# Three bias matmuls folded into the residual rows, and row and weight copies dropped, in a transformer kernel with linear attention

## The chip, the cores and the metric

The kernel runs as one program on 1 core of one Trainium2 chip. The metric is device time in microseconds (us), the median of several runs.

## What is computed

The input is 8 sequences of 512 tokens of width 128, in float32. An outer block modulates a layer norm of the input, runs a small transformer over it, and then a mixture of experts. The change touches the small transformer, which has four layers (16 heads of 8 features, feed-forward width 512) and is cut here to what matters:

```
for l in range(4):
    q, k, v = x @ Wq[l] + bq[l], x @ Wk[l] + bk[l], x @ Wv[l] + bv[l]
    att = causal_linear_attention(elu(q) + 1, elu(k) + 1, v)
          # (inter + intra) / (den_inter + den_intra + ATT_EPS), chunks of 128 tokens
    x = x + att @ Wo[l] + bo[l]
    x = layernorm(x) * g1[l] + be1[l]
    y = gelu(x @ W1[l] + b1[l]) @ W2[l] + b2[l]
    x = layernorm(x + y) * g2[l] + be2[l]
return layernorm(x) * gf + bef
```

None of the biases is zero. After it come a residual with a gate, a second modulated layer norm, a router over 16 experts with two chosen for each token, a shared expert and the weighted sum. That part is not changed except for one wait.

## The kernel before

**Tiles.** A tile is 128 tokens by 128 features. A row is one sequence: `NT` = 4 tiles. All 32 tiles of the residual stream stand in SBUF in `X`. There are `STEPS` = 32 pairs of a layer and a row. Every engine has its own program, unrolled by `steps`: it runs `body(k * NT)` for k = -1 to 34, and in one step k the work of four pairs is interleaved: the transposes of x for pair k+1 (`active(i, -1)`), projections and the first two attention tiles for pair k (`back` 0), the other attention tiles, the output projection and the first layer norm for pair k-1 (`back` 1), the first feed-forward matmul for pair k-2 (`back` 2), the second one and the second layer norm for pair k-3 (`back` 3). The first steps also carry the head (the modulated layer norm of the input, a row at a time, `dve_head_step` and its like), the last ones the tail.

**Order.** The order on each engine is written out by hand; between engines there are only semaphores (`wait(engine, sem, value)`).

**TensorE.** In a step its order is, twice over: `qkv`, `attend`, `qkv`, `att_transpose`, `ffn_out`, `project` (with the transposes of the row of pair k-2, L1208, ahead of the second one), and then, twice over: `ffn_in`, `attend`, `att_transpose`, `ffn_in`, `project` (with the transposes of pair k+1, L1254, after the first). Biases are added by matmuls of bfloat16: three rows of ones times the bias, split into three bfloat16 parts (`bias3`): L1135 for q, k and v, L1171 for the output projection, L1186 for the second feed-forward matmul. The epsilon of the denominator comes from a matmul of the same kind, L1151. L1147 is the cumulative sum over the tokens, six recorded passes of 384 columns.

**VectorE.** In each of a step's four parts it has `feature_map` (L1416, in parts 0 and 1 twice), `weigh` (L1422), `outputs` (L1431 to L1445), the residual additions (L1455, L1473) and the statistics. In parts 0 and 1 it has tiles n = 2 and n = 3 of pair k-1, in parts 2 and 3 tiles n = 0 and n = 1 of pair k. `outputs` reduces the products to `red`, adds the part from earlier tiles (L1440, `tot`), takes the reciprocal of the denominators (L1442, 16 values a token, into PSUM), and multiplies (L1445).

**GpSimd.** Per tile: the small steps of the first layer norm (L1071 to L1077), the outer products of k and v (`outer`, L1057, for tile n = part number), gain and shift (L1094, L1097); per step the second layer norm (L1084 to L1090, L1102, L1106). Its constants are built first (L1009 to L1047).

**ScalarE.** It evacuates PSUM (L1281 to L1297, L1332, L1366), does the exponential of the feature map (L1287), the GELU (L1310), the normalisations (L1316, L1323), and changes its function table twice a step (L1301).

**SyncE.** In each step it copies a row of `X` to `xs` (for L1254) and another to `x1s` (for L1208), and the layer's `w1` to `w1s` (for L1198), by DMA within SBUF, each behind waits for the rows. The one-time loads (`first_loads`) and the clearing of the experts' scratch stand between these copies, so their issue is held back by the same waits.

## Time and profile before

| | |
|---|---|
| median of 3 runs | 1248.11 us (1247.34 to 1251.08) |
| time of the profiled execution | 1249.31 us |
| span of the profiled execution | 1247.6 us |
| TensorE busy, matmuls | 969.0 us (78%) |
| VectorE busy | 841.5 us (67%) |
| GpSimd busy | 879.9 us (71%) |
| ScalarE busy | 573.0 us (46%) |
| granted TensorE clock, mean | 0.905 |

Busy shares are means over the whole span. The four layers take up the time to about 885 us, the router, experts and mixing the rest. Between about 137 us and 838 us the kernel repeats one step 28 times.

### The profile page before, as it was taken

How to read it: one execution, taken by the hardware profiler on the slowest of the kernel's cores; microseconds unless marked ns; L12 is line 12 of the kernel's file. 1: busy time of each engine (PE TensorE's matmuls, PEld its weight loads, DVE VectorE, ACT ScalarE, POOL GpSimd, SP SyncE). 2: the span in 40 equal slices, each digit the busy share in tenths (PEclk: the TensorE clock that was granted, in tenths of full speed). 3: DMA queues.
4: the chain of work that ended last, by engine and by line, in shares of the span. 5: the costliest groups of instructions: out<-in, count | busy, mean ns of one | idle time of the engine just before them, and what ended most of it. 6: DMA issues, size and time to landing. Idle time of an engine off the chain costs nothing.

```text
span 1247.6 us, 20239 instructions
## 1 busy us (share of the span) xinstructions
PE 969.0 (78%) x4916; PEld 653.8 (52%) x4916; DVE 841.5 (67%) x2224; ACT 573.0 (46%) x1441; POOL 879.9 (71%) x1262
## 2 busy tenths in 40 slices
PE   2768999999999999999999999997233955997000
PEld 0445566666666666666666666664232534775000
DVE  2788788888888888888888888884565432443223
ACT  2345565556565655565556555654441112332000
POOL 4678888878887888788878887885745778000775
PEclk9899999999999999999999999998655887999555
DMA  9511001000100010001000100000001222552222
GB/s 250 182 68 69 26 35 43 27 29 32 43 26 29 33 43 27 26 35 44 26 27 34 43 27 27 27 34 18 18 0 35 74 81 82 148 148 96 65 74 61
DMA packets 53541, 69.01 MB, mean 55 GB/s; under 512 B 12296, under 2 KB 30136, under 8 KB 53312
## 3 DMA queue, kind: packets, MB, share of 16 engines
q1 hardware_dynamic: 44814, 54.21, 13.2%
q0 software_dynamic: 4096, 8.40, 2.2%
q10 hardware_dynamic: 4530, 5.26, 1.2%
q8 instruction: 38, 0.62, 0.2%
q14 instruction: 63, 0.52, 0.1%
HBM read 24.03 MB, written 16.80 MB: 33 GB/s over the span
## 4 chain that ended last, share of the span: by engine, by line
POOL 19%; PE 15%; issue 13%; DVE 12%; ACT 4%; DMA 1%; POOLq 1%; DVEq 0%; SPq 0%; ACTq 0%
POOL expert_in_scratch L693 4%; POOL w L726 4%; DVE prod L1422 3%; PE ps L1147 3%; POOL kv L1057 3%; DVE red L1435 2%; PE ps L739 2%; POOL rstd L1074 2%; PE ps L737 1%; PE ps L788 1%; PE ps L789 1%; POOL rstd L1087 1%; PE ps L741 1%; PE ps L1136 1%; ACT hT L1310 1%
## 5 line engine op out<-in xcount | busy, mean ns | idle before, releaser
L1057 POOL TENSOR_TENSOR kv<-qk,v 128x1152 f32<-128x1152 f32 x128 | 280.8, 2194 | 3.1 <-DVE qk L1416 3.1
L1147 PE MATMUL ps<-kv,tri 128*128 128x384 f32 x768 | 272.9, 492 | 0.9 <-DVE prod L1422 0.7
L1422 DVE TENSOR_TENSOR prod<-ps,qk 128x1152 f32<-128x1152 f32 x128 | 173.3, 1354 | 61.9 <-PE ps L1147 61.9
L1147 PEld LDWEIGHTS ps<-kv,tri 128*128 128x128 f32 x768 | 137.7, 193 | 91.0 <-issue 19.0
L1435 DVE TENSOR_REDUCE red<-prod 128x144 f32<-128x1152 f32 x128 | 172.2, 1345 | 3.7 <-DVE prod L1422 0.5
L1198 PE MATMUL ps<-x1T,w1s 128*128 128x512 f32 x256 | 135.1, 610 | 4.8 <-ACT hT L1310 4.4
L1188 PE MATMUL ps<-w,hT 128*128 128x128 f32 x1024 | 138.8, 286 | 0.0
L1188 PEld LDWEIGHTS ps<-w,hT 128*128 128x128 f32 x1024 | 127.7, 196 | 1.5
L1136 PE MATMUL ps<-wqkv,xT 128*128 128x384 f32 x256 | 107.7, 503 | 0.0
L1281 ACT ACTIVATE rl<-ps 128x256 f32<-128x256 f32 x128 | 48.7, 381 | 126.1 <-PE ps L1136 126.1
L1416 DVE SCALAR_TENSOR_TENSOR qk<-ps,ex 128x256 f32<-128x256 f32 x128 | 53.9, 421 | 65.0 <-ACT ex L1287 63.2
L1310 ACT ACTIVATE hT<-ps,b1c 128x512 f32<-128x512 f32 x128 | 87.0, 680 | 22.6 <-PE ps L1198 22.6
L1316 ACT ACTIVATE xn<-y,shift,rstd 128x128 f32<-128x128 f32 x128 | 63.2, 494 | 66.4 <-POOL shift L1077 66.4
L693 POOL DMA_INDIRECT expert_in_scratch<-hs,idx_s x64 | 63.5, 992 | 24.2 <-issue 18.4
L726 POOL DMA_INDIRECT w<-expert_out_scratch,idx_s x64 | 63.6, 994 | 24.0 <-issue 17.4
L1074 POOL TENSOR_TENSOR rstd<-var,halfneg 128x1 f32<-128x1 f32 x128 | 72.4, 566 | 10.7
L1301 ACT ACT_TABLE_LOAD x60 | 77.0, 1283 | 1.1
L1071 POOL TENSOR_SCALAR var<-mv 128x1 f32<-128x1 f32 x128 | 28.7, 224 | 67.0 <-DVE mv L1482 58.7
L1097 POOL TENSOR_TENSOR X<-xg,gains 128x128 f32<-128x128 f32 x128 | 59.0, 461 | 18.3
L1135 PE MATMUL ps<-bias,ones 128*128 128x384 bf16 x128 | 42.7, 333 | 34.1 <-DVE qk L1416 33.2
L681 POOL COPY idx_s<-gath_u 128x8 uint32 (+1 forms) x8 | 1.6, 201 | 88.7 <-DMA expert_out_scratch<-kv 88.7
L1094 POOL TENSOR_TENSOR xg<-xn,gains 128x128 f32<-128x128 f32 x128 | 58.9, 460 | 6.3 <-ACT xn L1316 3.9
(220 smaller groups left out, 2202.0 us busy)
## 6 DMA issues: line engine op xcount, KB each, us to landing
x1s<-X SPq DMA_DIRECT2D x32, 256.0 KB, 2.3
w1s<-w SPq DMA_DIRECT2D x32, 256.0 KB, 2.5
xs<-X SPq DMA_DIRECT2D x31, 256.0 KB, 2.3
expert_in_scratch<-room SPq DMA_DIRECT2D x16, 320.0 KB, 3.5
kv<-expert_in_scratch SPq DMA_DIRECT2D x16, 320.0 KB, 3.1
expert_out_scratch<-kv ACTq DMA_DIRECT2D x16, 320.0 KB, 3.2
mod<-mod_scratch SPq DMA_DIRECT2D x1, 2304.0 KB, 9.0
x<-in_L_attn_x_dram SPq DMA_DIRECT2D x8, 256.0 KB, 5.9
```

What stands on the lines that cost most here:

```text
L693: pool.indirect_dma_start(out=xe_dram, out_offset=bass.IndirectOffsetOnAxis(ap=idx_s[:, par, 2 * n + k:2 * n + k + 1], axis=0), in_=hs2[:, ...
L726: pool.indirect_dma_start(out=yg[:, par, 2 * n + k, :], out_offset=None, in_=ye_dram, in_offset=bass.IndirectOffsetOnAxis(ap=idx_s[:, par, ...
L1057: pool.tensor_tensor(kv[:, n, :].rearrange("p (e h d) -> p e h d", e=EV, h=H), qk[:, n, 1, :].rearrange("p (h d) -> p h d", h=H).unsqueeze ...
L1074: pool.tensor_tensor(rstd1[:, par:par + 1], var1[:, par:par + 1], halfneg[:, 0:1], ALU.pow).then_inc(rstd1_ready, 1)
L1136: pe.matmul(ps_qkv, xT[:, n, :], wqkv[:, ds(layer, 1), :].rearrange("p a c -> p (a c)"), start=False, stop=True).then_inc(qkv_ps, 1)
L1147: mm = pe.matmul(ps_cum[:, j, :], tri[:, :], kv[:, n, j * CB:(j + 1) * CB], start=True, stop=True)
L1188: mm = pe.matmul(o, hT[:, j, n * P:(n + 1) * P], w2[:, ds(layer, 1), j, :].rearrange("p a c -> p (a c)"), start=False, stop=(j == FC - 1))
L1198: pe.matmul(ps_h, w1s[:, j * P:(j + 1) * P], x1T[:, :], start=True, stop=True).then_inc(h_ps, 1)
L1301: act.activation(table_use[:, :], csT[:, 0:1], function)
L1310: act.activation(hT[:, j, :], ps_h, ACT.Gelu, bias=b1c[:, ds(layer, 1), j]).then_inc(gelu_done, 1)
L1422: dve.tensor_tensor(prod[:, :].rearrange("p (b e c) -> p b e c", b=3, e=3), ps_cum.rearrange("p b (e c) -> p b e c", e=3), qk[:, n, 0, :]. ...
L1435: dve.tensor_reduce(red[:, :], prod[:, :].rearrange("p (c d) -> p c d", d=HD), AXX, ALU.add).then_inc(red_done, 1)
```

## The change

The epsilon matmul (L1151), the bias matmul of the output projection (L1171) and that of the second feed-forward matmul (L1186) are removed. Epsilon is added by a new VectorE instruction on the 16 denominators, between L1440 and L1442; for the first tile of a row, where nothing is added from earlier tiles, L1440 is removed instead. The two biases are carried in the residual rows: `bo` of layer 0 is added to the head's shift `mod`, `bo` of the later layers to the shift `gains[:, 3]` of the second layer norm, `b2` to the shift `gains[:, 1]` of the first. Since the same rows feed the projections, the bias is taken off again in the ScalarE copies out of the transposes (L1332, L1366), which become `Identity` with a per-partition bias. Four new loads bring the biases in, two of them as single elements onto partitions, two spread to all partitions. The transposes read `X` directly and `ffn_in` reads `w1` directly; the copies to `xs`, `x1s` and `w1s` are gone, and SyncE issues the one-time loads and the clearing one after another.

```diff
-        BR = 1 + 5 * L * D // 32
+        BR = 1 + 3 * L * D // 32
...
+        def tots_before(T):
+
+            return T - -(-T // NT)
...
             def dve_head_step(dve, j):
...
                 dve.wait_ge(mod01_loaded if b < 2 else mod_loaded, 16)
+                dve.wait_ge(resid_b_loaded, 32)
+                if b in (0, 2):
+                    rows_here = slice(b, 2 if b == 0 else B)
+                    count = 2 if b == 0 else B - 2
+                    dve.tensor_tensor(mod[:, rows_here, 0, :], mod[:, rows_here, 0, :],
+                                      resid_b[:, 0, 0:1, :].to_broadcast([P, count, D]), ALU.add).then_inc(bo_added, 1)
+                    dve.wait_ge(bo_added, 1 if b == 0 else 2)
...
# dve_route
+            if half == 0:
+                dve.wait_ge(q["xe_zeroed"], 16 * E)
...
# SyncE, step
-                if active(i, -1) and not is_first(i):
-                    wait_apart(sp, x_ready, i + 8, mod_stored)
-                    wait(sp, xt_ps, i + 4)
-                    row = tile_of(i, -1, 0)
-                    sp.dma_start(xs[:, :, :], X[:, ds(row, NT), :]).then_inc(xs_load, 16)
-                if isinstance(i, int) and i < NT * NT:
+                if i < NT * NT:
                     first_loads(i // NT)
-                if active(i, 2):
-                    wait_apart(sp, x1_ready, i - 4, mod_stored)
-                    wait(sp, x1t_ps, i - 8)
-                    row = tile_of(i, 2, 0)
-                    sp.dma_start(x1s[:, :, :], X[:, ds(row, NT), :]).then_inc(x1s_load, 16)
-                    wait(sp, h_ps, i - 8)
...
-                    sp.dma_start(w1s[:, :], w1[:, ds(layer_of(i, 2), 1), :].rearrange("p a f -> p (a f)")
-                                 ).then_inc(w1_load, 16)
...
# GpSimd
-            (five instructions that build eps3)
...
+            def residual_biases():
+
+                pool.wait_ge(par_loaded, 16 * 14)
+                pool.wait_ge(resid_b_loaded, 32)
+                pool.tensor_tensor(gains[:, 1, :, :], gains[:, 1, :, :], resid_b[:, 1, :, :], ALU.add).then_inc(resid_ready, 1)
+                pool.tensor_tensor(gains[:, 3, 0:L - 1, :], gains[:, 3, 0:L - 1, :], resid_b[:, 0, 1:L, :], ALU.add).then_inc(resid_ready, 1)
+                pool.wait_ge(resid_ready, 2)
...
-                if isinstance(i, int) and i == NT:
-                    pool.wait_ge(par_loaded, 16 * 14)
+                if i == NT:
+                    residual_biases()
...
# TensorE
-                mm = pe.matmul(ps_s[:, 0:SW], ones3[:, :], eps3[:, :], start=True, stop=(n == 0))
                 if n > 0:
                     wait(pe, kvm_ready, T)
-                    mm = pe.matmul(ps_s[:, 0:SW], qT[:, :], kvm[:, :], start=False, stop=True)
+                    mm = pe.matmul(inter, qT[:, :], kvm[:, :], start=True, stop=True)
...
-                pe.matmul(ps_y[:, 2 * D:3 * D], ones3[:, :], bias3_l[:, 3, ds(layer, 1), :] ..., start=True, stop=False)
...
-                    pe.matmul(o, ones3[:, :], bias3_l[:, 4, ds(layer, 1), :] ..., start=True, stop=False)
...
-                pe.matmul(ps_h, w1s[:, j * P:(j + 1) * P], x1T[:, :], start=True, stop=True).then_inc(h_ps, 1)
+                pe.matmul(ps_h, w1[:, layer_of(i, 2), j * P:(j + 1) * P], x1T[:, :], start=True, stop=True).then_inc(h_ps, 1)
...
-                        wait(pe, x1s_load, (i - 4) * 4)
+                        wait(pe, x1_ready, i - 4)
...
-                            mm = pe.transpose(ps_t[:, n * P:(n + 1) * P], x1s[:, n, :], ident[:, :])
+                            mm = pe.transpose(ps_t[:, n * P:(n + 1) * P], X[:, tile_of(i, 2, n), :], ident[:, :])
...
-                            mm = pe.transpose(ps_t[:, n * P:(n + 1) * P], source[:, n, :], ident[:, :])
+                            mm = pe.transpose(ps_t[:, n * P:(n + 1) * P], X[:, tile_of(i, -1, n), :], ident[:, :])
...
# ScalarE
-            for n, v in enumerate((bq, bk, bv, bo, b2)):
+            for n, v in enumerate((bq, bk, bv)):
...
+            for n, v in enumerate((bo, b2)):
+                act.dma_start(less_b[:, n, :], v.rearrange("l p -> p l"), allow_slow_non_contiguous=True).then_inc(less_b_loaded, 16)
+                act.dma_start(resid_b[:, n, :, :].rearrange("p l d -> p (l d)"),
+                              v.rearrange("(a l) d -> a (l d)", a=1).to_broadcast([P, L * D])).then_inc(resid_b_loaded, 16)
...
-                        act.activation(x1T[:, :], ps_t[:, :], ACT.Copy).then_inc(x1t_sb, 4)
+                        act.activation(x1T[:, :], ps_t[:, :], ACT.Identity, bias=less_b[:, 1, layer_of(i, 2):layer_of(i, 2) + 1]).then_inc(x1t_sb, 4)
...
+                        act.wait_ge(less_b_ready, 1)
                         (the copy to xT likewise, with less_b[:, 0, layer])
...
# VectorE
+            dve.wait_ge(less_b_loaded, 32)
+            dve.tensor_scalar(less_b[:, :, :], less_b[:, :, :], -1.0, None, ALU.mult).then_inc(less_b_ready, 1)
...
-                dve.tensor_tensor(tot[:, :, :].rearrange("p e h -> p (e h)"), red[:, :], ps_s[:, 0:SW], ALU.add).then_inc(tot_done, 1)
-                wait(dve, tot_done, T + 1)
-                dve.reciprocal(rden, tot[:, HD, :]).then_inc(rden_done, 1)
+                total = tot[:, :, :].rearrange("p e h -> p (e h)") if n > 0 else red[:, :]
+                if n > 0:
+                    dve.tensor_tensor(total, red[:, :], inter, ALU.add).then_inc(tot_done, 1)
+                    wait(dve, tot_done, tots_before(T + 1))
+                dve.tensor_scalar(rden, total[:, HD * H:SW], ATT_EPS, None, ALU.add).then_inc(den_done, 1)
+                wait(dve, den_done, T + 1)
+                dve.reciprocal(rden, rden).then_inc(rden_done, 1)
                 wait(dve, rden_done, T + 1)
```

## Rows read from the trace of the kernel before

**Rows 1.** Timeline of SyncE's queue: start, length (us), issue.
```profile
137.43 0.47 SPq L989 DMA_DIRECT2D x1s<-X  x1
...
837.59 0.46 SPq L989 DMA_DIRECT2D x1s<-X  x1
```

**Rows 2.** Busy time of the engines over the 28 repeated steps.
```profile
137.43:837.59 700.16, 674.85 (x3468) 450.33 (x3467) 576.85 (x1485) 420.27 (x1062) 575.94 (x842) 1.00 0.09 32
```

**Rows 3.** Chain that ended last, 440 to 500 us: start, length, what.
```profile
462.80 0.09 DVE qk L1416
...
466.92 0.43 DVE qk L1416
...
470.54 1.37 DVE prod L1422
...
476.27 0.23 POOL var L1071
...
487.70 0.09 DVE qk L1416
```

**Rows 4.** Timelines of DVE, PE, POOL, ACT; in brackets idle time before, and releaser.
```profile
487.70 0.42 DVE L1416 SCALAR_TENSOR_TENSOR qk<-ps,ex 128x256 f32<-128x256 f32 x1 [0.68 <-ACT ex L1287]
...
470.54 1.36 DVE L1422 TENSOR_TENSOR prod<-ps,qk 128x1152 f32<-128x1152 f32 x1 [0.43 <-PE ps L1147]
...
467.49 0.32 PE L1135 MATMUL ps<-bias,ones 128*128 128x384 bf16 x1 [0.26 <-DVE qk L1416]
...
488.27 0.32 PE L1135 MATMUL ps<-bias,ones 128*128 128x384 bf16 x1 [0.54 <-DVE qk L1416]
...
476.27 0.22 POOL L1071 TENSOR_SCALAR var<-mv 128x1 f32<-128x1 f32 x1 [1.94 <-DVE mv L1482]
...
484.15 0.49 ACT L1316 ACTIVATE xn<-y,shift,rstd 128x128 f32<-128x128 f32 x1 [0.54 <-POOL shift L1077]
```

**Rows 5.** Timeline of PE, one epsilon matmul and the matmul behind it.
```profile
470.34 0.23 PE L1151 MATMUL ps<-eps,ones 128*128 128x144 bf16 x1
470.40 0.46 PE L1154 MATMUL ps<-kvm,qT 128*128 128x144 f32 x2
```

**Rows 6.** Timeline of DVE: small dependent instructions, in a layer and in the router.
```profile
473.39 0.30 DVE L1440 TENSOR_TENSOR tot<-red,ps 128x144 f32<-128x144 f32 x1
473.73 0.26 DVE L1442 RECIPROCAL ps<-tot 128x16 f32<-128x16 f32 x1
...
935.06 0.17 DVE L632 TENSOR_SCALAR rsum<-rsum 128x16 f32<-128x16 f32 x1
935.27 0.25 DVE L633 RECIPROCAL rsum<-rsum 128x16 f32<-128x16 f32 x1
```

**Rows 7.** Timeline of ACT: copies out of PSUM.
```profile
479.20 0.60 ACT L1366 ACTIVATE xT<-ps 128x512 f32<-128x512 f32 x1
...
480.39 0.28 ACT L1292 ACTIVATE qT<-ps 128x128 f32<-128x128 f32 x1 [0.22 <-PE ps L1143]
```

**Rows 8.** Timelines of DVE and ACT in the head: waits for mod and for shift.
```profile
20.54 0.69 DVE L476 TENSOR_TENSOR X<-room,mod 128x512 f32<-128x512 f32 x1 [6.36 <-DMA mod<-mod_scratch]
...
57.46 0.49 ACT L1316 ACTIVATE xn<-y,shift,rstd 128x128 f32<-128x128 f32 x1 [3.17 <-POOL shift L1077]
```

**Rows 9.** Busy time by stretch: PE, PEld, DVE, ACT, POOL, clock, DMA share, GB/s.
```profile
8.00:10.00 2.00, 0.24 (x1) 0.00 (x0) 1.62 (x4) 1.35 (x2) 1.76 (x11) 1.00 1.20 290
...
52.00:56.00 4.00, 1.88 (x7) 1.06 (x7) 3.93 (x9) 1.04 (x4) 3.84 (x5) 0.75 0.00 0
```

**Rows 10.** Groups of instructions: xcount | busy us, mean ns | idle before.
```profile
L617 DVE TENSOR_TENSOR room<-room,rsum 128x256 f32<-128x256 f32 x2 | 0.9, 426 | 0.1
L482 DVE TENSOR_TENSOR X<-X,mod 128x512 f32<-128x512 f32 x8 | 5.5, 686 | 0.1
L1106 POOL TENSOR_TENSOR X<-xg,gains 128x512 f32<-128x512 f32 x29 | 37.0, 1276 | 4.9 <-POOL xg L1102 4.9
```

**Rows 11.** Timeline of PE in the head: a wait, and the matmul behind it.
```profile
86.10 0.32 PE L1135 MATMUL ps<-bias,ones 128*128 128x384 bf16 x1 [1.04 <-DVE qk L1416]
```

More of the change, by code:

```diff
@@ L28 @@
 BIAS = NB + 2 * D
-def bf16_parts(value):
-    parts, rest = [], np.float32(value)
-    for _ in range(3):
-        bits = rest.view(np.uint32)
-        part = np.uint32((int(bits) + 0x7FFF + ((int(bits) >> 16) & 1)) & 0xFFFF0000).view(np.float32)
-        parts.append(float(part))
-        rest = np.float32(rest - part)
-    return parts
 def wait(engine, sem, value):
@@ L134, in adaln_block_kernel @@
         xs = sb("xs", [P, NT, D])
-        x1s = sb("x1s", [P, NT, D])
-        w1s = sb("w1s", [P, FF])
         xT = sb("xT", [P, NT, P])
@@ L942, in _ @@
             sp.wait_ge(bias_split, 3)
-            sp.wait_ge(consts_ready, 19)
+            sp.wait_ge(consts_ready, 18)
             for r in range(3):
@@ L1022, in _ @@
                                base=HD - 1, pattern=[[0, EV], [HD, H]], channel_multiplier=-1).then_inc(consts_ready, 1)
-            lead, middle, last = bf16_parts(ATT_EPS)
-            then(pool.memset(eps3[:, :], 0.0))
-            then(pool.memset(eps3[0:3, :], lead))
-            for r, part in ((1, middle), (2, last)):
-                then(pool.affine_select(out=eps3[0:3, :], in_=eps3[0:3, :], compare_op=ALU.is_gt, fill=part, base=r,
-                                        pattern=[[0, SW]], channel_multiplier=-1))
-            pool.affine_select(out=eps3[0:3, :], in_=eps3[0:3, :], compare_op=ALU.is_ge, fill=0.0, base=-HD * H,
-                               pattern=[[1, SW]], channel_multiplier=0).then_inc(consts_ready, 1)
             for a in (swg[:, F:P + HB], swg[:, P + HB + FB:2 * P], ewg[:, :, F:P + HB], ewg[:, :, P + HB + FB:2 * P]):
@@ L1123, in _ @@
             mm.then_inc(mod_ps, 1)
-            pe.wait_ge(consts_ready, 19)
+            pe.wait_ge(consts_ready, 18)
             def qkv(i, n):
@@ L1170, in project @@
                 layer = layer_of(i, back)
-                pe.matmul(ps_y[:, 2 * D:3 * D], ones3[:, :], bias3_l[:, 3, ds(layer, 1), :].rearrange("r a c -> r (a c)"), start=True, stop=False)
-                pe.matmul(ps_y[:, 2 * D:3 * D], attT[:, :], wo[:, ds(layer, 1), :].rearrange("p a c -> p (a c)"), start=False, stop=True
+                pe.matmul(ps_y[:, 2 * D:3 * D], attT[:, :], wo[:, ds(layer, 1), :].rearrange("p a c -> p (a c)"), start=True, stop=True
                           ).then_inc(wo_ps, 1)
@@ L1185, in ffn_out @@
                     o = ps_y[:, m * D:(m + 1) * D]
-                    pe.matmul(o, ones3[:, :], bias3_l[:, 4, ds(layer, 1), :].rearrange("r a c -> r (a c)"), start=True, stop=False)
                     for j in range(FC):
                         mm = pe.matmul(o, hT[:, j, n * P:(n + 1) * P], w2[:, ds(layer, 1), j, :].rearrange("p a c -> p (a c)"),
-                                       start=False, stop=(j == FC - 1))
+                                       start=(j == 0), stop=(j == FC - 1))
                     mm.then_inc(w2_ps, 1)
@@ L1243, in step @@
                     if s == 0 and active(i, -1):
-                        source = X if is_first(i) else xs
-                        if is_first(i):
-                            pe.wait_ge(x_ready, NT)
-                        else:
-                            wait(pe, xs_load, (i + 4) * 4)
+                        wait(pe, x_ready, i + 8)
                         if active(i, 1):
@@ L1365, in step @@
                         wait(act, qkv_ps, i + 4)
-                        act.activation(xT[:, :, :].rearrange("p n t -> p (n t)"), ps_t[:, :], ACT.Copy).then_inc(xt_sb, 4)
+                        act.wait_ge(less_b_ready, 1)
+                        act.activation(xT[:, :, :].rearrange("p n t -> p (n t)"), ps_t[:, :], ACT.Identity, bias=less_b[:, 0, layer_of(i, -1):layer_of(i, -1) + 1]).then_inc(xt_sb, 4)
                     if active(i, 1) and s == 0:
```

27 lines of the change are left out of this document (16 added, 11 removed).

## The prediction

> **What bounds the kernel now.** I first looked for the repeating unit. The copy of `x1s` is issued once a step; its first and last rows in the regular stretch stand 700.16 us apart, 28 steps, so a step takes 25.0 us [rows 1]. In that stretch TensorE is recorded busy 674.85 us, 96%, VectorE 576.85, GpSimd 575.94 and ScalarE 420.27 [rows 2]. By that view TensorE is the bound. But matmul records overlap, so a nearly full TensorE does not prove it. I therefore read the chain that ended last. It goes round a ring once a step, from 462.80 to 487.70 [rows 3]: VectorE's `feature_map`, `weigh` and `outputs` for tile n = 2; `feature_map` at 466.92; TensorE with projection, transpose and cumulative sum up to 470.54; VectorE with `weigh` and `outputs` for tile n = 3, the residuals and statistics up to 476.27; GpSimd with the small norm steps, an outer product, both norms and a shift; ScalarE with norm, GELU, table load, evacuation and exponential; and VectorE's `feature_map` again at 487.70. That is 24.9 us.
>
> Is that ring the true bound, or only one path among many? At each handoff the receiver had been idle: VectorE 0.68 us for ScalarE, TensorE 0.26 us for VectorE, VectorE 0.43 us for TensorE, GpSimd 1.94 us for VectorE, ScalarE 0.54 us for GpSimd [rows 4]. So nobody else on the ring was late; whatever lengthens the ring lengthens the step, and whatever lies outside it has slack. TensorE's own slack shows as its waits for `qk`: 0.26 and 0.54 us in one step [rows 4].
>
> **The change part by part.**
>
> *Matmuls removed.* Per step 4 epsilon, 4 output-projection and 4 second-feed-forward bias matmuls. The epsilon matmul starts at 470.34 and the next at 470.40 [rows 5], so one costs 0.06 us of TensorE's stream, whatever its recorded 0.23. Twelve make 0.7 us a step. On the ring TensorE has only the stretch from 467.49 to 470.54, and in it run L1135 (kept), the projection, the transpose and L1147: none of the twelve. I value them at nothing. If TensorE were the bound, they would be worth 0.7 x 28 = 20 us.
>
> *The new denominator addition.* Per tile with n > 0 one `tensor_scalar` of 128x16 with its own wait goes between L1440 and L1442. The nearest row is L632 in the router: same operation, same shape, and its dependent reciprocal starts 0.21 us later [rows 6]. From above I bound it by L1440, whose dependent follows after 0.34 us [rows 6]; below, by 0.17, the busy time of L632 alone. I take 0.205, as operation and shape agree. The ring holds `outputs` of n = 2 and of n = 3, so 0.41 us a step, and 28 x 0.41 = 11.5 us. For n = 1 the addition stands outside the ring and is covered by VectorE's 0.68 us of idle time before 487.70 [rows 4]; with that cover gone it would cost another 0.2. For n = 0 the addition replaces the dearer L1440 (saves 0.13), also outside the ring.
>
> The addition writes PSUM and the reciprocal now reads it, where it read SBUF. The row of L1440, with one PSUM source, shows 0.30 us for 144 elements a partition, and it would be hard to find a penalty in it. The Trainium skill (VectorE: DVE Perf Modes, section on the TRN2 errata) gives a fixed 120 cycles at 0.96 GHz for a PSUM source against 58 for SBUF. That would be an estimated 0.065 us more for each reciprocal, 3.6 us over 56 of them on the ring; the sum would be that much higher.
>
> *Copies with a bias.* L1332 and L1366 become `Identity` with a per-partition operand. An `Identity` of 128x128 with two such operands takes 0.49 us [rows 4], a copy of the same shape 0.28 [rows 7], so 0 to 0.2 us for one operand, and I take 0.1. Neither is on the ring. The copy to `xT` (0.60 us [rows 7]) gates the tile n = 1, which is behind the same 0.68 us of VectorE's idle time; the removed matmuls ahead of it give back 0.2. So nothing; without that cover it would be 0.1 a step, 3 us. The Trainium skill (ScalarE: Activation LUTs, section on what ACT_TABLE_LOAD costs) puts a pointer operand at about 93 ns, and the two rows agree.
>
> *Copies by DMA removed.* No handoff on the ring waits for one. The transposes now wait for the rows directly; `x1_ready` comes from GpSimd's previous step. Nothing. SyncE now issues its one-time loads and the clearing without waits; order in its queue is unchanged, and what is cleared is written 900 us before it is used. Nothing. The new wait in the router finds it done.
>
> *The head.* Four terms. (a) The first rows wait 6.36 us for `mod` to come back from memory [rows 8], and its store is issued when the DMA engines are full at 290 GB/s [rows 9]. Two spread loads of 256 KB in ScalarE's queue add 0.5 MB, at that rate 1.8 us; below, nothing, if they fill gaps. With the single-element loads beside them I take 1.3. (b) Behind that wait `bo` is added to two rows, 128x256: 0.43 us [rows 10] plus a dependent start of 0.03: 0.5. (c) In step 0 the same for six rows, 128x768: by the two shapes of rows 10 about 0.96, with the wait 1.0; VectorE is busy 3.93 of 4 us after it [rows 9], so it shifts all that follows. (d) At the start of step 1 GpSimd gets two additions of 128x512 and 128x384 and waits for them: 1.28 [rows 10] and three quarters of it, with the waits 2.4. Behind them stands the shift for which ScalarE waits 3.17 us [rows 8], and behind it `feature_map` and TensorE. So 2.4. Removed GpSimd constants and a shorter `bias3` end before the wait for `mod` and give nothing. Together 5.2 us, between 3.5 and 6.
>
> *Head steps and drain.* In steps 1 to 3 the chain passes `outputs` of n = 3 and n = 1, 0.4 us each, and in step 0 0.1: 1.3 us. In the drain one addition is on the chain, and some bias matmuls leave it: 0.1.
>
> **Sum.** 11.5 + 5.2 + 1.3 + 0.1 = 18.1 us. The profiled execution took 1249.31 us (its span 1247.6), 1.2 over the median of 1248.11. 1249.31 + 18.1 = 1267.4, and against the median 1266.
>
> **The rivals.**
>
> *TensorE is the bound.* For it: 96% busy [rows 2]. Then every step loses 0.7 us and the additions hide: 1248.1 - 20 + 5.2 = about 1234. It decides if TensorE's slack in a step, 0.8 us by its waits, is not there, that is if `qk` only looks late. Against it: TensorE waits for `qk` twice, and those waits are the handoffs of the ring. Chance 0.08.
>
> *The additions are absorbed* by slack that I don't see, such as VectorE waiting anyway for TensorE in `weigh` (0.43 us [rows 4]). Then the head alone counts: 1253. Against it: that wait follows upon the late `qk` of tile n = 2 and moves with it. 0.10.
>
> *The addition is dear:* 0.34 us each, by L1440, instead of 0.205: 28 x 2 x 0.34 = 19, 2.1 in the head steps, and 5.3: 1274.5. The rule on PSUM sources lies in this direction, at 1270 by its figure. 0.12.
>
> *TensorE's clock falls.* With fewer matmuls in a longer step, its wait at 488.27 grows from 0.54 to about 1.3 us. In the head a wait of 1.04 us left a 128x384 matmul at 0.32 us, the length at the full 2.4 GHz [rows 11], while a stretch in which it was busy 1.88 of 4 us had a granted clock of 0.75 [rows 9], part of it at 1.2 GHz. If it fell in each step for one pass of L1147, 1.95 us at full clock by its starts in the chain, 28 x 1.95 = 55 us more: 1321. It decides from waits between 1.04 and about 2 us. 0.06.
>
> **How the numbers follow.** My own case has 0.64. With the bounds of its costs (head 3.5 to 6, addition 0.17 to 0.25, the `xT` copy 0 to 3) it runs from 1262 to 1271. To leave out no more than 2 in 10 the range takes in the absorbed and the dear case: 1252 to 1277. About 0.3%, 3.7 us, is what a measurement of this kernel can tell from no change. Faster by more: only the TensorE case, 0.08. Within it: the low end of the absorbed case, 0.03. Slower: 0.89.
>
> **What would show each step.** The regular step should be 25.4 us, not 25.0 or 24.3. The new instruction should stand 0.2 us ahead of its reciprocal. TensorE's waits for `qk` should grow to more than 1.5 us a step, with the clock still 1.00, and its busy time fall. The first L476 should start near 22 us and have 0.5 us ahead of it; two additions of 2.4 us should stand before L1071 in step 1. The prediction is wrong if the step gets shorter, which would mean that a removed matmul or copy was on the ring, or if the additions show up as less idle time before `feature_map` or `weigh` instead of a longer step.

## The result and the profile after

The changed kernel takes 1269.17 us (median of 4 runs, 1268.70 to 1270.78), the kernel before 1248.36 us (4 runs, 1247.34 to 1251.08). The ratio is 1.0167, with a 95% interval of 1.0151 to 1.0183: slower by 20.8 us. Forecast were 1266 us and a range of 1252 to 1277.

The profiled execution took 1269.35 us (span 1267.6), 20.0 us more than that of before. To see where they arose I need a mark that stands in both kernels once a step. ScalarE's copy of `x1T` is one. Timeline of ScalarE, kernel before: steps 4, 32 and 33.

```profile
143.10 0.58 ACT L1332 ACTIVATE x1T<-ps 128x512 f32<-128x512 f32 x1
...
842.04 0.58 ACT L1332 ACTIVATE x1T<-ps 128x512 f32<-128x512 f32 x1
...
864.16 0.57 ACT L1332 ACTIVATE x1T<-ps 128x512 f32<-128x512 f32 x1
```

The same of the changed kernel, which answers to [rows 1] as well:

```profile
150.95 0.67 ACT L1320 ACTIVATE x1T<-ps,less_b 128x512 f32<-128x512 f32 x1
...
861.64 0.67 ACT L1320 ACTIVATE x1T<-ps,less_b 128x512 f32<-128x512 f32 x1
...
884.41 0.66 ACT L1320 ACTIVATE x1T<-ps,less_b 128x512 f32<-128x512 f32 x1
```

Subtract the rows in pairs. At step 4 the changed kernel is 7.85 us late, at step 32 19.60, at step 33 20.25. From there to the end of the span both need 383.2 to 383.4 us, the changed kernel 0.25 less. So there are two losses and no others of size: 7.85 us in the head, and 11.75 us in 28 regular steps (24.96 to 25.38 us each, 0.42 a step). A mark is read from one execution. In kernels 3, 6 and 8 below the mark of step 4 stands 1.25 to 1.5 us earlier than in the kernel before, with edits that the sum prices at nothing there. So I take a mark at the end of the head as good to about 1.5 us, and the 7.85 with it. The length of the regular step is far firmer, as such an error is spread over 28 steps.

**The regular step.** Busy time between the two marks, PE, PEld, DVE, ACT, POOL, clock, DMA share and GB/s, answers to [rows 2]:

```profile
150.95:861.64 710.69, 645.09 (x3125) 429.69 (x3123) 588.19 (x1571) 423.68 (x1058) 572.96 (x840) 1.00 0.00 1
```

TensorE's share has fallen from 96% to 91%, and the step is longer. So TensorE doesn't bound the changed kernel; whether it bounded the kernel before, kernel 3 will say. The DMA engines carry next to nothing any more (32 GB/s before, 1 now), and no time came of it. The granted clock is 1.00: full speed, 2.4 GHz, through all 28 steps.

The timeline of VectorE shows the new instruction on the ring; it answers to the first two of [rows 6] and to the first of [rows 4].

```profile
487.24 0.30 DVE L1433 TENSOR_TENSOR tot<-red,ps 128x144 f32<-128x144 f32 x1
487.57 0.18 DVE L1435 TENSOR_SCALAR ps<-tot 128x16 f32<-128x16 f32 x1
487.79 0.27 DVE L1437 RECIPROCAL ps<-ps 128x16 f32<-128x16 f32 x1
488.09 0.29 DVE L1440 TENSOR_TENSOR att<-tot,ps 128x128 f32<-128x128 f32 x1
...
476.43 0.42 DVE L1407 SCALAR_TENSOR_TENSOR qk<-ps,ex 128x256 f32<-128x256 f32 x1 [1.20 <-ACT ex L1275]
...
483.53 0.42 DVE L1407 SCALAR_TENSOR_TENSOR qk<-ps,ex 128x256 f32<-128x256 f32 x1 [0.88 <-ACT ex L1275]
...
502.03 0.42 DVE L1407 SCALAR_TENSOR_TENSOR qk<-ps,ex 128x256 f32<-128x256 f32 x1 [1.49 <-ACT ex L1275]
```

Before, `tot` and the reciprocal started 0.34 us apart. Now the addition starts 0.33 after `tot` and the reciprocal 0.22 after the addition. So 0.21 us went in, with no idle gap around it. The idle time ahead of the first `feature_map`, 0.68 us in [rows 4], is now 1.2 to 1.5 us (476.43 and 502.03, one step apart). The additions of tiles n = 0 and 1 had their cover, and the cover grew; kernel 5 tests it.

Waits between step 4 and step 32 (us in total, times, longest), kernel before:

```profile
DVE prod L1422 <- PE ps L1147: 56.4, 84, 1.0
...
DVE qk L1416 <- ACT ex L1287: 43.7, 54, 1.4
...
PE ps L1135 <- DVE qk L1416: 22.0, 54, 0.8
```

and changed:

```profile
DVE qk L1407 <- ACT ex L1275: 56.8, 53, 1.5
...
DVE prod L1413 <- PE ps L1137: 38.3, 82, 0.7
...
PE ps L1125 <- DVE qk L1407: 37.5, 54, 0.8
```

TensorE waits for `qk` 1.34 us a step where it waited 0.79. VectorE waits for TensorE 0.65 us a step less. Kernel 3 below, which only leaves matmuls out, shows how much of this is theirs. There TensorE's wait for `qk` is 1.12 us a step, 0.33 more than before. VectorE's wait for TensorE is 0.44 less, and its wait for `ex` 0.39 more. So the removed matmuls bought a TensorE that is ready earlier and an equal wait elsewhere; the rest of the 1.34 comes with the longer step.

Groups of instructions between the two marks (count, busy us, mean ns), changed kernel:

```profile
L1437 DVE RECIPROCAL ps<-ps 128x16 f32<-128x16 f32 x112 | 29.8, 266 | 3.9
...
L1320 ACT ACTIVATE x1T<-ps,less_b 128x512 f32<-128x512 f32 x28 | 19.2, 686 | 1.1 <-PE ps L1196 0.8
...
L1435 DVE TENSOR_SCALAR ps<-tot 128x16 f32<-128x16 f32 x84 | 14.9, 178 | 2.9
```

and the two of before that have a counterpart:

```profile
L1442 DVE RECIPROCAL ps<-tot 128x16 f32<-128x16 f32 x112 | 29.2, 261 | 3.8
...
L1332 ACT ACTIVATE x1T<-ps 128x512 f32<-128x512 f32 x29 | 17.3, 596 | 8.7 <-PE ps L1208 8.6
```

The reciprocal went from 261 to 266 ns when its source moved to PSUM, 5 ns. The Trainium skill (VectorE: DVE Perf Modes, section on the TRN2 errata) has 120 fixed cycles against 58, from which I had estimated 65 ns; the trace doesn't agree. (The page's row is for a result in SBUF, and this reciprocal writes PSUM in both kernels.) The copies with a bias went from 596 to 686 ns, 90 ns, against the forecast 0.1 us. The Trainium skill (ScalarE: Activation LUTs, section on what ACT_TABLE_LOAD costs) has 93 ns for a pointer operand, and here the trace agrees.

**The head.** Timelines of VectorE, TensorE and GpSimd in the changed kernel; they answer to [rows 8], [rows 10] and, with the row at 91.94, to [rows 11].

```profile
21.74 0.43 DVE L477 TENSOR_TENSOR mod<-mod,resid_b 128x256 f32<-128x256 f32 x1 [5.84 <-DMA mod<-mod_scratch]
22.20 0.69 DVE L480 TENSOR_TENSOR X<-room,mod 128x512 f32<-128x512 f32 x1
...
40.44 0.96 DVE L477 TENSOR_TENSOR mod<-mod,resid_b 128x768 f32<-128x768 f32 x1 [1.09 <-ACT room L463]
41.44 0.69 DVE L480 TENSOR_TENSOR X<-room,mod 128x512 f32<-128x512 f32 x1
...
48.72 1.36 DVE L1413 TENSOR_TENSOR prod<-ps,qk 128x1152 f32<-128x1152 f32 x1 [1.38 <-PE ps L1137]
...
45.18 3.50 PE L1137 MATMUL ps<-kv,tri 128*128 128x384 f32 x6 [2.39 <-DVE prod L1413]
...
91.94 0.48 PE L1125 MATMUL ps<-bias,ones 128*128 128x384 bf16 x1 [1.02 <-DVE qk L1407]
...
93.71 3.77 PE L1137 MATMUL ps<-kv,tri 128*128 128x384 f32 x6
...
60.09 1.27 POOL L1038 TENSOR_TENSOR gains<-gains,resid_b 128x512 f32<-128x512 f32 x1
61.32 1.00 POOL L1039 TENSOR_TENSOR gains<-gains,resid_b 128x384 f32<-128x384 f32 x1
62.41 0.23 POOL L1061 TENSOR_SCALAR var<-mv 128x1 f32<-128x1 f32 x1
```

and of the kernel before (TensorE, VectorE, GpSimd):

```profile
36.25 4.04 PE L1147 MATMUL ps<-kv,tri 128*128 128x384 f32 x6
...
42.45 2.17 PE L1147 MATMUL ps<-kv,tri 128*128 128x384 f32 x6
...
70.19 2.17 PE L1147 MATMUL ps<-kv,tri 128*128 128x384 f32 x6 [0.74 <-DVE prod L1422]
...
38.71 0.69 DVE L476 TENSOR_TENSOR X<-room,mod 128x512 f32<-128x512 f32 x1 [1.09 <-ACT room L466]
...
44.66 1.36 DVE L1422 TENSOR_TENSOR prod<-ps,qk 128x1152 f32<-128x1152 f32 x1
...
56.09 0.24 POOL L1071 TENSOR_SCALAR var<-mv 128x1 f32<-128x1 f32 x1
```

Follow one delay from row to row. `mod` is ready at 21.74 instead of 20.54: 1.20. Behind the two-row addition the first scaling starts 1.66 late, so that is 0.46. The six-row addition takes 0.96 and a start: the scaling behind it begins at 41.44 instead of 38.71, which adds 1.07. Then comes something that I had not foreseen. The cumulative sum L1137 waits 2.39 us and then takes 3.50 us, where it took 2.17: the granted clock over these 3.50 us is 0.60, so a good part of its six passes ran at half clock. That is 1.33 us, and the next `prod` starts 4.06 us late. GpSimd's two additions bring the delay of `var` to 6.32 us.

Up to step 4 another 1.5 us is added, but not evenly. The marks of steps 2, 3 and 4 are 5.63, 7.53 and 7.85 us late. Nearly all of the growth, 1.90 us, lies between the marks of steps 2 and 3, and there the granted clock is 0.81 where the kernel before has 0.94. The row at 91.94 is the counterpart of [rows 11]: a wait of 1.04 us was followed by 0.32 us at full clock, and here a wait of 1.02 is followed by 0.48 us and then by a cumulative sum of 3.77 us instead of 2.16.

### The profile page after: what moved, and what is told of

It reads as the page before. It is cut to its first block and busy times, and to the rows that moved or that the text cites. A ratio compares the mean times of both kernels' runs of the same rounds, so it can differ in the third digit from the quotient of the medians.

```text
span 1267.6 us, 19443 instructions
## 1 busy us (share of the span) xinstructions
PE 935.1 (74%) x4532; PEld 630.5 (50%) x4532; DVE 855.5 (67%) x2323; ACT 578.2 (46%) x1441; POOL 878.2 (69%) x1259
## 5 line engine op out<-in xcount | busy, mean ns | idle before, releaser
L1137 PE MATMUL ps<-kv,tri 128*128 128x384 f32 x768 | 274.9, 495 | 2.4 <-DVE prod L1413 2.4
L1137 PEld LDWEIGHTS ps<-kv,tri 128*128 128x128 f32 x768 | 138.8, 194 | 95.3 <-issue 27.3
L1186 PE MATMUL ps<-x1T,w 128*128 128x512 f32 x256 | 135.7, 612 | 9.0 <-ACT hT L1298 4.3
L1175 PE MATMUL ps<-w,hT 128*128 128x128 f32 x1024 | 127.0, 278 | 5.0 <-issue 4.3
L1175 PEld LDWEIGHTS ps<-w,hT 128*128 128x128 f32 x1024 | 121.1, 194 | 17.6 <-issue 17.6
L1304 ACT ACTIVATE xn<-y,shift,rstd 128x128 f32<-128x128 f32 x128 | 63.1, 493 | 66.6 <-POOL shift L1067 66.6
L1160 PEld LDWEIGHTS ps<-wo,attT 128*128 128x128 f32 x256 | 41.5, 192 | 69.4 <-issue 65.5
L1160 PE MATMUL ps<-wo,attT 128*128 128x128 f32 x256 | 52.6, 288 | 27.6 <-issue 27.1
L1311 ACT ACTIVATE xn<-y,shift,rstd 128x128 f32<-128x128 f32 x128 | 52.7, 482 | 41.5 <-POOL shift L1080 41.5
```

Of the source, the lines that this page charges most:

```text
L1137: mm = pe.matmul(ps_cum[:, j, :], tri[:, :], kv[:, n, j * CB:(j + 1) * CB], start=True, stop=True)
L1160: pe.matmul(ps_y[:, 2 * D:3 * D], attT[:, :], wo[:, ds(layer, 1), :].rearrange("p a c -> p (a c)"), start=True, stop=True).then_inc(wo_ps, 1)
L1175: mm = pe.matmul(o, hT[:, j, n * P:(n + 1) * P], w2[:, ds(layer, 1), j, :].rearrange("p a c -> p (a c)"), start=(j == 0), stop=(j == FC - 1))
L1186: pe.matmul(ps_h, w1[:, layer_of(i, 2), j * P:(j + 1) * P], x1T[:, :], start=True, stop=True).then_inc(h_ps, 1)
```

## The experiments

Times are medians; each ratio is to the kernel before measured beside it on the same chip, with its 95% interval. "Step" is the distance of the `x1T` marks from step 4 to step 32, divided by 28; "mark" is the one of step 4 (143.10 us before, 150.95 changed). Both are read from one profiled execution of each kernel.

| kernel | us | ratio | step | mark |
|---|---|---|---|---|
| before | 1248.4 | 1 | 24.96 | 143.10 |
| changed | 1269.2 | 1.0167 (1.0151 to 1.0183) | 25.38 | 150.95 |
| 1 changed, epsilon by matmul | 1254.2 | 1.0035 (1.0018 to 1.0053) | 24.90 | 147.75 |
| 2 before, epsilon on VectorE | 1263.8 | 1.0105 (1.0078 to 1.0131) | 25.34 | 147.18 |
| 3 before, bias matmuls left out | 1248.1 | 1.0001 (0.9990 to 1.0012) | 24.94 | 141.67 |
| 4 changed, one more, n = 2, 3 | 1284.1 | 1.0282 (1.0250 to 1.0314) | 25.83 | 150.52 |
| 5 changed, one more, n = 0, 1 | 1272.3 | 1.0181 (1.0154 to 1.0208) | 25.41 | 149.37 |
| 6 before, copies removed | 1248.9 | 1.0014 (0.9997 to 1.0031) | 24.94 | 141.85 |
| 7 changed, denominators first | 1255.9 | 1.0064 (1.0044 to 1.0084) | 24.99 | 148.40 |
| 8 before, norm later | 1250.0 | 1.0005 (0.9978 to 1.0032) | 24.74 | 141.62 |
| 10 = 7 with norm later | 1252.3 | 1.0032 (1.0019 to 1.0046) | 24.59 | 146.02 |
| 11 changed, head moved | 1268.2 | 1.0167 (1.0144 to 1.0189) | 25.36 | 149.30 |
| 12 = 10 with the head of 13 | 1246.8 | 0.9986 (0.9973 to 0.9999) | 24.56 | 145.73 |
| 13 changed, head placed anew | 1266.9 | 1.0144 (1.0127 to 1.0161) | 25.40 | 146.56 |

In kernels 10 and 12 the step from mark 4 to mark 5 takes 26.97 and 26.08 us; the other 27 average 24.50 in both, against 25.01 in kernel 7.

**1 and 2: the denominator addition, taken out and put in alone.**

```diff
# 1, on the changed kernel (2 is the reverse, on the kernel before)
+                mm = pe.matmul(ps_s[:, 0:SW], ones3[:, :], eps3[:, :], start=True, stop=(n == 0))
...
-                dve.tensor_scalar(rden, total[:, HD * H:SW], ATT_EPS, None, ALU.add).then_inc(den_done, 1)
-                wait(dve, den_done, T + 1)
-                dve.reciprocal(rden, rden).then_inc(rden_done, 1)
+                dve.reciprocal(rden, tot[:, HD, :]).then_inc(rden_done, 1)
```

> The changed kernel with the epsilon matmul and the old denominator path put back; everything else of the change stays. Theory (the additions of n = 2 and n = 3 lie on a ring through VectorE, GpSimd, ScalarE and TensorE, and TensorE has slack): the regular step goes back from 25.38 to 24.96 us, 28 x 0.42 = 11.8 and 1.3 in the head steps less: about 1256. Rival (TensorE is the bound): four matmuls of 0.06 us more a step, 28 x 0.24 = 7 more: 1276.

> The kernel before with the denominator part alone: epsilon matmul removed, addition of epsilon on VectorE. Theory (ring): 1248.4 + 11.8 + 1.3 = about 1261. Rival (the addition hides in VectorE's waits and the loss comes from the other parts): 1248. Rival (TensorE is the bound): 1241.

With the matmul back, the step is 24.90 us: the whole growth of the step is gone, with eight of the twelve bias matmuls still removed. With the addition alone it is 25.34, nearly all of the growth. So the step's loss is this one instruction. Kernel 2 is 3 us slower than expected, and that lies in the head: its mark is 4.1 us late where I had 1.3 for the additions. Its timeline of TensorE shows what is there.

```profile
58.81 3.90 PE L1141 MATMUL ps<-kv,tri 128*128 128x384 f32 x6
...
71.54 3.07 PE L1141 MATMUL ps<-kv,tri 128*128 128x384 f32 x6 [1.17 <-DVE prod L1415]
...
90.03 3.66 PE L1141 MATMUL ps<-kv,tri 128*128 128x384 f32 x6
```

The granted clock over these three groups is 0.54, 0.68 and 0.57. From 45 us on the kernel before has one such group, at 58.13 (3.44 us, clock 0.61). Near 36 us both kernels have a long one (4.04 and 3.17 us), for which the profile gives a clock of 1.00, so I don't count it. Against 2.17 us the three cost 1.7, 0.9 and 1.5 us and the one of before 1.3. That is 2.8 more, and with the 1.3 of the additions it makes the 4.1; that all of it lies on the path is not shown.

Together the two kernels split the head. Kernel 1 has all four head terms and no addition, and its mark is 4.65 us late; kernel 2 has the additions alone, and its mark is 4.1 late. So of the 7.85 us the additions took 3.2 (from kernel 1 to the changed one) to 4.1, where the sum had 1.3, and the four terms 3.8 to 4.65, where it had 5.2. The place is the same in every kernel: with an addition between `tot` and the reciprocal (changed, 2, 4, 5, 11, 13) the step from mark 2 to mark 3 takes 30.1 to 31.1 us, and in all others 28.3 to 29.0. The sum had 0.4 for that. Half clock is only a part of it, since in 4, 5 and 13 the granted clock there is 0.94, as before; the rest is open.

**3 and 6: the other two parts alone.**

```diff
# 3, on the kernel before: the bias matmuls left out, epsilon for n = 0 only
-                pe.matmul(ps_y[:, 2 * D:3 * D], ones3[:, :], bias3_l[:, 3, ...], start=True, stop=False)
-                    pe.matmul(o, ones3[:, :], bias3_l[:, 4, ...], start=True, stop=False)
-                mm = pe.matmul(ps_s[:, 0:SW], ones3[:, :], eps3[:, :], start=True, stop=(n == 0))
+                if n == 0:
+                    mm = pe.matmul(ps_s[:, 0:SW], ones3[:, :], eps3[:, :], start=True, stop=True)
# 6, on the kernel before: the reads of the copies, and with them the copies
-                            mm = pe.transpose(ps_t[:, n * P:(n + 1) * P], x1s[:, n, :], ident[:, :])
+                            mm = pe.transpose(ps_t[:, n * P:(n + 1) * P], X[:, tile_of(i, 2, n), :], ident[:, :])
```

> The kernel before with the matmuls removed and nothing put in their place: it leaves out both biases, and epsilon for all tiles but the first of a row (11 of the 12 matmuls a step). Theory (TensorE has slack): regular step unchanged, drain up to 1 us less: 1247 to 1248. Rival (TensorE is the bound): 11 x 0.06 x 28 = 18 less: 1230.

> The kernel before with only the copies to xs, x1s and w1s removed: transposes read X, ffn_in reads w1, SyncE issues loads and clearing without waits. Theory: no wait on the ring is for a copy, so 1248, within 0.3%. Rival (the clearing, now in one burst, or reads of X by TensorE disturb the head or the steps): slower by 2 us or more.

Both give what was expected: nothing. Eleven matmuls fewer a step make the step 0.02 us shorter, and so does the removal of the copies, which is within what single steps differ. (In both profiled executions the mark of step 4 is earlier, by 1.4 and 1.25 us, and the step from mark 32 to mark 33 longer by 1.6, with a cumulative sum of 3.8 us in it instead of 2.2. How much of this is the edit's and how much the execution's, one trace of each kernel doesn't say.) The rival in which TensorE is the bound falls here. Only the sum's zero for both terms was at stake, and it holds.

**4 and 5: one more instruction of the same kind, on the ring and off it.**

```diff
                 wait(dve, den_done, T + 1)
+                if n >= 2:      # 5: n < 2
+                    dve.tensor_scalar(rden, rden, 0.0, None, ALU.add).then_inc(more_done, 1)
+                    done_more[0] += 1
+                    wait(dve, more_done, done_more[0])
```

> The changed kernel with one more dependent instruction of the same size (adds 0.0 to the 16 denominators) in outputs for tiles n = 2 and n = 3 only. Theory (ring): both lie on it, 2 x 0.21 x 28 = 11.8, and about 1 in head and drain: 1282. Rival (VectorE has so much slack that a share is absorbed): under 1275.

> The same extra instruction, in outputs for tiles n = 0 and n = 1 only: as many instructions as in the run before it. Theory (ring): VectorE's idle time of 0.95, 0.67 and 0.68 us covers them, so nothing in the regular steps and 0.2 us in each of three head steps (n = 1): 1270. Rival (VectorE's total busy time counts, wherever it stands): 1282, as for n = 2 and 3.

On the ring the step grew by 0.45 us, 0.22 for each. Off it, by 0.03 for two of the same instruction. In time it is 14.9 against 3.1 us, by the ratios 14.4 against 1.7. Of the 3.1 us only 0.9 lies in the 28 regular steps. The same work in the same engine costs fifteen times more or less in a regular step by its place alone. So the ring that I read from the chain of waits is the ring.

**7: the denominators first.** The extra instruction costs its full length since `tot`, addition and reciprocal each wait for the one before. A kernel that adds the denominators by themselves, before the rest of `tot`, leaves `tot` to run while the denominators are on their way.

```diff
-                    dve.tensor_tensor(total, red[:, :], inter, ALU.add).then_inc(tot_done, 1)
-                    wait(dve, tot_done, tots_before(T + 1))
-                dve.tensor_scalar(rden, total[:, HD * H:SW], ATT_EPS, None, ALU.add).then_inc(den_done, 1)
+                    dve.scalar_tensor_tensor(out=rden, in0=red[:, HD * H:SW], scalar=ATT_EPS, in1=inter[:, HD * H:SW],
+                                             op0=ALU.add, op1=ALU.add).then_inc(den_done, 1)
+                    dve.tensor_tensor(total[:, 0:HD * H], red[:, 0:HD * H], inter[:, 0:HD * H], ALU.add).then_inc(tot_done, 1)
```

> The changed kernel with the denominators first: for n > 0 one instruction forms (red + epsilon) + inter on the 16 denominators straight from red, then the other 128 columns of tot, then the reciprocal, so that two of the three dependent starts fall away. Nothing is left out. Theory: the chain from red to att is as long as before the change or up to 0.05 us longer, so the regular step is 24.9 to 25.1 us and the time 1256 to 1260. Rival (it is the number of instructions that counts, not their dependent starts): 1269.

1255.9 us, 13 us better than the changed kernel. The timeline of VectorE shows how:

```profile
472.20 0.17 DVE L1433 SCALAR_TENSOR_TENSOR ps<-red,ps 128x16 f32<-128x16 f32 x1
472.28 0.28 DVE L1435 TENSOR_TENSOR tot<-red,ps 128x128 f32<-128x128 f32 x1
472.48 0.26 DVE L1439 RECIPROCAL ps<-ps 128x16 f32<-128x16 f32 x1
472.83 0.29 DVE L1444 TENSOR_TENSOR att<-tot,ps 128x128 f32<-128x128 f32 x1
```

From the first start to that of `att` it takes 0.63 us; in the changed kernel, 487.24 to 488.09, it took 0.85. `tot` starts 0.08 us after the addition, since it doesn't need its result, and the reciprocal 0.20 after `tot`. The same number of instructions, none of them shorter by more than 0.02 us, costs 0.22 us less, and the step, which has two of them on its ring, got 0.39 shorter: 10.9 us in 28 steps. Another 2.5 is the earlier mark, 148.40 instead of 150.95.

**8 and 10: shorten the ring elsewhere.** ScalarE's norm of a tile stands on the ring ahead of the GELU and the table load. Put behind them, it leaves the ring.

```diff
-                    if active(i, 1) and s == 1:
-                        norm1(i + s - 2, s % 2)
                     if active(i, 2):
                         gelu(i, 2 * s + 1)
                     if s == 1 and active(i, 0) and active(i, 2):
                         fetch_table(ACT.Exp)
+                    if active(i, 1) and s == 1:
+                        norm1(i + s - 2, s % 2)
```

> The kernel before with one thing changed, outside the studied change: on ScalarE the normalisation of part 3 (L1316) is issued behind the last GELU and the table load instead of ahead of them. Nothing is left out. Theory (the ring goes from GpSimd's shift over this normalisation to GELU and table load): the GELU starts when its matmul is done, about 0.8 us earlier, and 0.4 comes back when the normalisation runs ahead of the evacuation: regular step 24.96 to about 24.55 us, 28 x 0.4 = 11: 1237. Rival (TensorE was the bound all along, the ring only looks critical): 1248.

> The changed kernel with the denominators first (as in the run of that name) and the normalisation behind the table load. Theory: the same 0.4 us a step off the time of the kernel with the denominators first: 1256 - 11 = 1245. Second theory: once the part over GpSimd is out of the ring, TensorE's stream is next, and then the 0.7 us of removed matmuls a step begin to count: regular step 24.2 instead of 24.55, down to 1235. Rival (the ring is not shortened): 1256.

On the kernel before the step fell by 0.22, about half of what was expected. On kernel 7 it fell by 0.40, as expected (0.50 without the first step). The profile of kernel 8 is of an execution of 1241.8 us, one of its four shortest, so the 0.22 is shown for that one only. Chain of waits of kernel 8, 480 to 540 us, its first line (shares by line):

```profile
by line: PE ps L1147 21.8%; issue 16.5%; PE ps L1198 12.4%; PE ps L1188 6.3%; PE ps L1136 5.4%; DVE prod L1422 4.5%; DVE qk L1416 3.7%; ACT L1301 3.1%; ACT xn L1316 2.4%; ACT ex L1287 2.2%; PE ps L1135 2.2%; PE ps L1154 2.0%; PE ps L1172 1.
```

and its busy time in the regular steps, PE first:

```profile
150.00:840.00 690.00, 670.32 (x3451) 449.82 (x3450) 572.70 (x1471) 412.14 (x1049) 569.85 (x838) 1.00 0.09 32
```

TensorE has 59% of the chain in this stretch now, where it had 10% in the kernel before, with lines such as L1198 and L1188 that were no part of the ring, and it is busy 97%. I read these lines so: once the ring is 0.2 us shorter, TensorE bounds the kernel before. Kernel 10 has twelve matmuls fewer a step, and there the edit brings its 0.4. By this reading the matmuls' removal is worth something after all, but only to who shortens the ring too. No run isolates it: kernels 7 and 10 differ from before and 8 in the copies and the denominators as well, and kernel 8 with the matmuls left out was not run.

Neither is a faster kernel all the same. The twelve times of kernel 8 are four up to 1243.7 us, two near 1247 and six from 1252.3 to 1254.5, and one profile doesn't say what parts them. Kernel 10 is at 1252 instead of the expected 1245. Of its gain at mark 4, 2.4 us before kernel 7, nothing is left at mark 5: the cumulative sum at 147.07 took 4.06 us, and the granted clock from 140 to 150 us is 0.79, where kernel 7 has 1.00. At the last row's first feed-forward matmul it is 11.9 us ahead of kernel 7, and by the medians only 3.7. Most of the rest was given back in the drain, where few matmuls are left. Timeline of TensorE for that row in kernel 7, a first pair and the last group:

```profile
871.59 1.12 PE L1186 MATMUL ps<-x1T,w 128*128 128x512 f32 x2 [1.21 <-ACT x1T L1320]
...
882.20 2.02 PE L1175 MATMUL ps<-w,hT 128*128 128x128 f32 x16 [0.73 <-DVE y L1454]
```

in kernel 10:

```profile
859.69 2.08 PE L1186 MATMUL ps<-x1T,w 128*128 128x512 f32 x2 [4.20 <-ACT x1T L1320]
862.54 2.08 PE L1186 MATMUL ps<-x1T,w 128*128 128x512 f32 x2 [0.78 <-ACT hT L1298]
...
871.15 3.75 PE L1175 MATMUL ps<-w,hT 128*128 128x128 f32 x16 [0.82 <-issue]
875.63 3.75 PE L1175 MATMUL ps<-w,hT 128*128 128x128 f32 x16 [0.73 <-DVE y L1454]
```

and a stretch of kernel 10 (the clock is third from the end):

```profile
860.00:864.00 4.00, 3.22 (x4) 0.69 (x3) 2.06 (x10) 0.69 (x1) 0.00 (x0) 0.50 0.00 0
```

Kernel 7 waits 1.21 us and keeps its clock. Kernel 10 waits 4.20 us, and then four pairs take 2.08 us each instead of 1.12 and both groups of sixteen 3.75 instead of 2.02, at a granted clock of 0.50. That is 4 x 0.96 + 2 x 1.73 = 7.3 us. By the rows the lead shrinks from 11.9 us to 4.84, since the last group ends at 884.22 and at 879.38. The Trainium skill (TensorE: Matmul & The Clock Gate, Part 1, section "What's actually happening") has 1.2 GHz as the level of an idle TensorE; the trace agrees, with 0.50 of 2.4 GHz behind the 4.20 us of waiting.

**11, 13 and 12: the head.**

```diff
# 11: GpSimd's additions into step 0, part 2; the six-row addition one head step earlier
-                if i == NT:
-                    residual_biases()
                 for s in range(4):
+                    if i == 0 and s == 2:
+                        residual_biases()
# 13: into step 0, part 1, ahead of the head's row; one small addition before mod is stored
+                    if i == 0 and s == 1:
+                        residual_biases()
...
+            act.dma_start(bo8[:, :], bo[0:1, :].to_broadcast([B, D])).then_inc(bo_added, 16)
...
+            then(dve.tensor_tensor(m3[:, 0, 0, :], m3[:, 0, 0, :], bo8[:, :], ALU.add))
```

> The changed kernel with two of the head's additions moved into idle time: GpSimd's two sums of gains from the start of step 1 to part 2 of step 0, and the sum for six rows of mod to the end of the head step before, where VectorE waits 2.85 us for ScalarE. Theory: 2.4 and 1.0 us less, and the steps in the regular stretch unchanged: 1269.2 - 3.4 = about 1266. Rival (the head's additions were covered anyway, and the 6.3 us by which step 1 starts late came from the loads): 1269.

Kernel 11 missed. The shift came 2.65 us earlier in step 1, but the additions now stood ahead of an outer product, and TensorE waited for that:

```profile
52.09 4.21 PE L1141 MATMUL ps<-kv,tri 128*128 128x384 f32 x6 [2.56 <-POOL kv L1051]
```

A group that takes 2.17 us at full clock took 4.21, at a granted clock of 0.50: half clock again. Of what was moved, 1.65 us was left at step 4, and the ratio is that of the changed kernel.

> The changed kernel with its head placed in another way, nothing else: the six- and two-row additions of bo to the shift are replaced by one small addition on 8 partitions before the shift is stored; the two spread loads go from ScalarE's queue to SyncE's; GpSimd's two additions stand in step 0, in the part before the head's row instead of at the start of step 1. The regular step must stay at 25.4 us. If the head terms (mod late, two-row and six-row additions, GpSimd's additions, and the pass at halved clock after them) cost what the trace of the changed kernel shows, 5 to 6 us of the head come back, less about 1 for the new small addition: the step-4 mark near 146 instead of 150.95, time 1264 to 1265. If, as in the two kernels that moved head work so far, another wait takes their place, the mark stays at 148 to 150 and the time at 1267 to 1269.

Kernel 13 has its mark at 146.56: 4.4 us of the head came back, and the profiled execution, span 1263.4 us, keeps 4.2 of them to the end. So more than half of the 7.85 us of the head came of how and where the additions and the loads were put (the two large additions to the shift are one small one now), not of carrying the biases as such. Its median, 1266.9, is 2.3 us below that of the changed kernel and 2 to 3 above the expected.

> As the run before it, and with the head's costs taken out: bo of layer 0 is added to the 8 rows of mod8 ahead of their store (one instruction on 8 partitions in place of 128x256 and 128x768), the two spread loads stand in SyncE's queue behind the gains instead of beside the first rows, and GpSimd's two sums stand in its idle time between its second outer product and the head step of step 0. Theory: 1.2 + 0.5 - 0.3 of the first rows, 1.0 + 1.3 of step 0 with the lower clock, 2.3 of step 1, so 5 to 6 us less than the run before it: 1239 by the first theory, 1230 by the second. Rival (as the first attempt to move these sums showed, another wait takes their place): 1 to 2 us less.

Kernel 12 has both. It is faster than the kernel before by 0.14%, which is no difference by the 0.3% of the prediction, and it missed both of the numbers expected. Its mark is only 0.3 us before that of kernel 10, though kernel 13 won 4.4 by the same edit; between 60 and 120 us its clock is 0.83 to 0.95. Part of it can be read: the cumulative sum at 43.88 us took 3.76 us in kernel 12, and its counterpart in kernel 10 took 2.17 at 44.71, behind a wait of 1.93 us. That is 1.6 us. Why the head keeps the rest of the gain in one kernel and not in the other is open.

## Why the prediction was right

**The bound.** The ring, not TensorE. Shown by kernels 3, 4 and 5: in the regular step work off the ring is free, whether taken away (3) or added (5), and work on it costs its length. As I read kernel 8, TensorE was next, some 0.2 us a step behind, closer than the 0.8 us of slack that the prediction took from its waits; that is not shown by a run of its own.

**Matmuls and copies removed: nothing.** Kernels 3 and 6 measured nothing, in time and in the step. The price of 0.06 us a matmul was not put to the test; the busy time of TensorE fell. Its waits for `qk` grew less than the prediction said would show: to 1.34 us a step, not over 1.5, and none to 1.3, the longest being 0.8.

**The addition: 11.5 us, measured 11.75.** Taken as 0.205 from a row of the router of the same operation and shape, it is 0.21 by the timeline, and kernel 4 gives 0.22. Taken out of the changed kernel (1) it is worth 0.48 us a step, put into the kernel before (2) 0.38. The dear case, 0.34, falls with it, and so does the penalty for a PSUM source. The additions of n = 0 and 1 stayed under VectorE's idle time, as did the longer copies.

**The head: 5.2 and 1.3 us, measured 7.85 together.** Up to `var` in step 1 the four terms came out at 1.20, 0.46, 1.07 and 2.26 us, 4.99 in all: (a) 1.3, (b) 0.5, (c) 1.0 and (d) 2.4 were right to 0.15 each. What was missing there is TensorE's clock in step 0, 1.33 us. I had a rival for the clock, but only for the regular steps, where it stayed at 1.00. I had read [rows 9] and [rows 11] as an answer for those steps and not asked what 2.4 us of extra waiting would do in the head. The bound drawn from [rows 11], that the clock stands a wait of 1.04 us, is wrong as well: waits of 1.02 (the changed kernel, 91.94) and 0.74 us (kernel 7, 76.42) were followed by half clock.

That steps 1 to 3 brought 1.5 for the 1.3 of the additions is in good part luck. By the marks of kernels 1 and 2 the additions cost 3.2 to 4.1 us in the head, and the four terms only 3.8 to 4.65 when followed to step 4. So the term of 1.3 was sized too small and that of 5.2 too large, and the two errors partly cancel. The excess of the additions sits between marks 2 and 3, and why it is so much larger there than 0.4 us is open.

**The drain: 0.1, measured 0.4**, which is 0.65 from step 32 to step 33 and 0.25 back after it. It is less than the 1.6 us by which that step differs between kernel 3 or 6 and the kernel before.

So the sum, 18.1, is 1.9 below the 20.0 that marks and span show: 1.35 in the head, 0.25 in the regular steps and 0.3 in the drain. The 1.35 has the size of the clock's term in step 0, but it is also within the 1.5 us to which a mark is good. The bounds that the prediction lists for its own case (head up to 6, addition up to 0.25, `xT` copy up to 3) add up to 1272.5, not to 1271; the range of 1252 to 1277 holds either.

## What to carry to other kernels

Find the ring first, and price an edit by where it stands on it: here twelve matmuls off it were worth nothing, and two instructions of 0.18 us on it cost 12 us. If something must be added on it, break its dependence: put it beside an instruction that runs anyway, not between two that wait for each other. And where the matmuls are sparse, in head and drain, look at the granted clock of the matmuls behind each new wait, and compare more than one execution before a microsecond there is put down to an edit.

## What was not expected of the hardware

- Six passes of 384 columns took up to 4.21 us in the head instead of 2.17, and two of 512 columns 2.08 in the drain instead of 1.12, at granted clocks down to 0.50. The wait just before doesn't tell when. The kernel before waited 0.74 us at 70.19 and took 2.17 us, and kernel 10 waited 1.93 at 44.71 and took 2.17. Kernel 7 waited 0.74 as well:

```profile
76.42 3.87 PE L1137 MATMUL ps<-kv,tri 128*128 128x384 f32 x6 [0.74 <-DVE prod L1413]
```

- From 155 to 830 us the granted clock is 1.00 in every kernel here, with TensorE busy 90% (kernel 4) to 97% (kernel 8). In kernels 10 and 12 half clock still came once behind mark 4, with 4.06 and 3.85 us for the six passes.
- What the clock costs isn't proportional to a delay: kernel 10 reached the drain 12 us earlier than kernel 7 and lost 7 of them there.
- A reciprocal of 128x16 takes 266 ns from PSUM and 261 from SBUF.
- An independent VectorE instruction starts 0.08 us after one of 0.17 us, a dependent one 0.22 us after one of 0.18.
